# State space stage: half of the product with C taken by GpSimd in some of the states

## The chip, the cores and the metric

The kernel is one program on one core of one Trainium2 chip. The metric is the device time of one execution in microseconds, the median of the runs taken. One further execution was profiled; its span runs from the first to the last instruction, and its own device time is a little longer than the span.

## The reference, cut to what matters

The model is a decoder of four layers with twelve parts (attention, cross attention and feed forward in each). The part that the change touches is the attention of layer 2, a selective state space model on 64 sequences of 64 tokens, with 256 inner channels and N = 16 states per channel:

```
delta = softplus(dt @ w_dt)
deltaA = exp(delta[..., None] * A)
deltaBu = delta[..., None] * B[:, :, None, :] * u[..., None]
step(h, (a, bu)):  h = a * h + bu
y = einsum('bldn,bln->bld', hs, C) + u * D
out = (y * silu(res)) @ w_out
```

`y` is a sum over the 16 states of `hs * C`, where `C` is one row (a value per token and state) that is the same for all channels. The other eleven parts are not changed.

## The kernel before, in words

The twelve parts run one after the other as stages. The stage `state_space` (L2353 and on) has the channels on the 128 partitions, in two halves `c` = 0 and 1, and the tokens along the free dimension, in 8 groups `g` of GT = 512 tokens (NG = 8). Its main loop runs over M = 8 x 16 = 128 steps `m`, one for each group and state; `k = m % 16` is the state, and below "k = 4" means the step of that state in any group. All tiles are float32.

For each step and half the work is a chain over four engines:

- TensorE spreads the row of B over the partitions (`b_row`, into one PSUM bank) and the row of C (`c_row`, into two banks in turn), both at L2434.
- ScalarE copies the row of B into SBUF (`copy_b`, L2580, tile `bs`) and computes the decay exp(delta * A) of each half into a PSUM bank (`decay`, L2591).
- GpSimd multiplies `du` with the copied row of B (`inputs`, L2653, tile `bu`), once for each half.
- VectorE runs the recurrence (`scan`, L2716, tile `hs`) and multiplies its result with the row of C out of PSUM (`contribute`, L2724, tile `hc`), once for each half.
- TensorE adds `hc` over the 16 states in PSUM by multiplying with the identity (`accumulate`, L2456, two passes over float32).

GpSimd cannot be handed the row of C as it is, since that lies in PSUM; only `bs` is in SBUF. `bu`, `hs` and `hc` have two buffers each, by `m % 2`. So a scan of step m waits for the product of m - 2, a product waits for the sum of m - 2, and `c_row(m + 1)` waits until the products of step m - 1 have been taken. `decay(m + 1, c)` writes the bank that `scan(m, c)` reads and waits for it.

The order on each engine is written out by hand. In step m:

- TensorE: `accumulate(m-1, 0)`, `b_row(m+2)`, `c_row(m+1)`, `accumulate(m-1, 1)`, then work for other groups by k: at k = 0 to 3 the convolution of the next group (L2407, four matmuls in a step), at k = 4 the output projection of the group before (`output`, L163), at k = 5 and 6 two input projections (L2398), at k = 7 and 8 `projected` (L2417), at k = 9 and 10 `step_size` (L2425), at k = 13 a transposition, at k = 14 and 15 input projections.
- ScalarE: `decay(m+1, 0)`, `copy_b(m+2)`, `decay(m+1, 1)`, then by k: copies out of the shared bank, at k = 6 `silus` with a table load, at k = 9 to 11 the softplus with a table load, at k = 12 the scaling of a later group.
- GpSimd: `inputs(m+1)` for both halves, then at k = 2 `gated` (L2666), at k = 8 the norm of a later group (L661 to L673), at k = 9 `parts` (L2675 to L2680), at k = 12 `step_size` (L2658 and L2661, 1024 wide).
- VectorE: at k = 1 `skipped` of the group before (L2729), at k = 5 `residual` of the group before (L2734, waits for `output`), then `scan(m, 0)`, `contribute(m-1, 1)`, at k = 9 `below_high` (L2709), `scan(m, 1)`, `contribute(m, 0)`, at k = 7 statistics.

The work on later groups falls away in the last groups: group 6 has no norm, scaling, transposition or input projections of its own to prepare, and group 7 prepares nothing.

Of the kernel before, what the change touches and what calls it, by code (L numbers as in the profile page):

```python
# [18 lines left out]
ALU = mybir.AluOpType  # L19
# [7 lines left out]
GT = NT * P  # L27
# [2325 lines left out]
def state_space(nc, e, W):  # L2353

    N = 16
    M = NG * N
    use = ssm_order()  # L2360
    names = PN_SEMS + ("zeroed misc_mm misc_cp taps_done u_done res_done hi_done parts_own bc_parts relu_done sp_own sp_done "
                       "nb_raw nb_done dl_done du_done b_mm c_mm b_cp a_done bu_done hs_done hc_done acc_mm yo_done yr_done")
    with block_of(nc, "state_space", names) as (block, s):
        room = Room(e.arena)
        u_b, res_b, delta_b, du_b = (room.pair(2 * GT) for _ in range(4))
        u, res, delta, du = (lambda g, c, t=t: t(g)[:, c * GT:(c + 1) * GT] for t in (u_b, res_b, delta_b, du_b))
        bs = room.pair(GT)
        bu_t, hs_t, hc_t = (room.take(4 * GT) for _ in range(3))
        bu, hs, hc = (lambda m, c, t=t: t[:, (2 * (m % 2) + c) * GT:(2 * (m % 2) + c + 1) * GT] for t in (bu_t, hs_t, hc_t))
        xp_all, raw_u = room.take(2 * NB * (S + 3)), room.take(2 * GT)  # L2370
# [10 lines left out]
        @block.tensor  # L2381
        def _(pe):
            def take(step, g):
                if use[step, g] >= 1:
                    pe.wait_ge(s["misc_cp"], use[step, g])

            def turn(g):
                take("ln", g)
                for j in range(NT):
                    pe.wait_ge(s["ln_xn"], NT * g + j + 1)  # L2390
                    ins = pe.transpose(misc[:, j * P:(j + 1) * P], xn[:, j * D:(j + 1) * D], e.ident)
                ins.then_inc(s["misc_mm"], 1)

            def channels(step, g):
                m = int(step[1])
                take(step, g)
                pe.wait_ge(s["misc_cp"], use["ln", g] + 1)
                pe.matmul(misc, W("w_in")[:, m * P:(m + 1) * P], xnT, start=True, stop=True).then_inc(s["misc_mm"], 1)  # L2398

            def convolve(c, g, which):  # L2400
                if which[0] == 0:
                    take(("cv0", "cv1")[c], g)
                    pe.wait_ge(s["misc_cp"], use[("m0", "m1")[c], g] + 1)
                    if g == 0:
                        pe.wait_ge(s["taps_done"], 1)
                for i in which:
                    ins = pe.matmul(tiles(misc, NB), taps(c, i), xp(c)[:, :, i:i + S],  # L2407
                                    start=(i == 0), stop=(i == 3))
                if which[-1] == 3:
                    ins.then_inc(s["misc_mm"], 1)  # L2410

            def projected(step, g):
                k, lo, p0 = {"dt": (64, 0, 0), "bc": (32, 64, 64)}[step]
                take(step, g)
                pe.wait_ge(s["u_done"], 2 * (g + 1))
                for c in range(2):
                    ins = pe.matmul(misc[p0:p0 + k, :], W("w_x")[:, c * 96 + lo:c * 96 + lo + k], u(g, c),  # L2417
                                    start=(c == 0), stop=(c == 1))
                ins.then_inc(s["misc_mm"], 1)

            def step_size(step, g):
                c = int(step[1])
                take(step, g)
                pe.wait_ge(s["misc_cp"], use["dt", g] + 1)
                pe.matmul(misc, W("w_dt")[:, c * P:(c + 1) * P], dts, start=True, stop=True).then_inc(s["misc_mm"], 1)  # L2425

            def output(g):
                take("y", g)
                pe.wait_ge(s["yr_done"], 2 * (g + 1))
                project_out(pe, e, misc, [(u(g, c), W("w_out")[:, c * D:(c + 1) * D]) for c in range(2)],  # L2430
                            None).then_inc(s["misc_mm"], 1)

            def row_of(out, g, row):
                return pe.matmul(out, e.sel[:, row:row + 1].broadcast_to([96, P]), bcp(g), start=True, stop=True)  # L2434

            def b_row(m):
                if m < M:
                    pe.wait_ge(s["bc_parts"], m // N + 1)
                    if m >= 1:
                        pe.wait_ge(s["b_cp"], m)  # L2440
                    row_of(bbank, m // N, m % N).then_inc(s["b_mm"], 1)

            def c_row(m):
                if m < M:
                    pe.wait_ge(s["bc_parts"], m // N + 1)
                    if m >= 2:
                        pe.wait_ge(s["hc_done"], 2 * m - 2)
                    row_of(cbank(m), m // N, N + m % N).then_inc(s["c_mm"], 1)

            def accumulate(m, c):  # L2450
                if m >= 0:
                    g, k = m // N, m % N
                    if k == 0 and g >= 1:
                        pe.wait_ge(s["yo_done"], 2 * (g - 1) + c + 1)
                    pe.wait_ge(s["hc_done"], 2 * m + c + 1)
                    pe.matmul(acc(c), e.ident, hc(m, c), start=(k == 0), stop=(k == N - 1)).then_inc(s["acc_mm"], 1)  # L2456

            turn(0)
            channels("m0", 0)
            channels("m1", 0)  # L2460
            for c in range(2):
                convolve(c, 0, range(4))
            channels("m2", 0)
            channels("m3", 0)
            projected("dt", 0)
            projected("bc", 0)
            step_size("d0", 0)
            step_size("d1", 0)
            b_row(0)
            b_row(1)  # L2470
            c_row(0)
            turn(1)
            channels("m0", 1)
            channels("m1", 1)
            for m in range(M):
                g, k = m // N, m % N
                accumulate(m - 1, 0)
                b_row(m + 2)
                c_row(m + 1)
                accumulate(m - 1, 1)  # L2480
                if k == 4 and g >= 1:
                    output(g - 1)
                if g + 1 < NG:
                    if k < 4:
                        convolve(k // 2, g + 1, ((0, 1), (2, 3))[k % 2])
                    if k in (5, 6):
                        channels(("m2", "m3")[k - 5], g + 1)
                    if k in (7, 8):
                        projected(("dt", "bc")[k - 7], g + 1)
                    if k in (9, 10):  # L2490
                        step_size(("d0", "d1")[k - 9], g + 1)
                if g + 2 < NG:
                    if k == 13:
                        turn(g + 2)
                    if k in (14, 15):
                        channels(("m0", "m1")[k - 14], g + 2)
            accumulate(M - 1, 0)
            accumulate(M - 1, 1)
            output(NG - 1)

        @block.scalar
        def _(a):
# [72 lines left out]
            def copy_b(m):  # L2575
                if m < M:
# [2 lines left out]
                        a.wait_ge(s["bu_done"], 2 * (m - 1))  # L2579
                    a.activation(bs(m), bbank, ACT.Copy).then_inc(s["b_cp"], 1)  # L2580

            def decay(m, c):
                if m < M:
                    g, k = m // N, m % N
# [29 lines left out]
            for m in range(M):  # L2614
                g, k = m // N, m % N
                decay(m + 1, 0)
                copy_b(m + 2)
                decay(m + 1, 1)
                if g + 1 < NG:
                    if k in (1, 3):  # L2620
# [22 lines left out]
        def _(q):  # L2643
            def inputs(m):
                if m < M:
                    g, k = m // N, m % N
                    q.wait_ge(s["b_cp"], m + 1)
                    for c in range(2):
                        if k == 0:
                            q.wait_ge(s["du_done"], g + 1)  # L2650
                        if m >= 2:
                            q.wait_ge(s["hs_done"], 2 * (m - 2) + c + 1)
                        q.tensor_tensor(bu(m, c), du(g, c), bs(m), ALU.mult).then_inc(s["bu_done"], 1)  # L2653

            def step_size(g):
                q.wait_ge(s["relu_done"], 2 * (g + 1))
# [32 lines left out]
            for m in range(M):  # L2689
                g, k = m // N, m % N  # L2690
                inputs(m + 1)
                if k == 2 and g >= 1:
                    gated(g - 1)
                if k == 12 and g + 1 < NG:
# [9 lines left out]
        def _(v):  # L2704
# [6 lines left out]
            def scan(m, c):  # L2711
                v.wait_ge(s["a_done"], 2 * m + c + 1)
                v.wait_ge(s["bu_done"], 2 * m + c + 1)
                if m >= 2:
                    v.wait_ge(s["hc_done"], 2 * (m - 2) + c + 1)
                v.tensor_tensor_scan(hs(m, c), at(c), bu(m, c), 0.0, ALU.mult, ALU.add).then_inc(s["hs_done"], 1)  # L2716

            def contribute(m, c):
                if m >= 0:
                    v.wait_ge(s["hs_done"], 2 * m + c + 1)  # L2720
                    v.wait_ge(s["c_mm"], m + 1)
                    if m >= 2:
                        v.wait_ge(s["acc_mm"], 2 * (m - 2) + c + 1)
                    v.tensor_tensor(hc(m, c), hs(m, c), cbank(m), ALU.mult).then_inc(s["hc_done"], 1)  # L2724

            def skipped(g):
                for c in range(2):
                    v.wait_ge(s["acc_mm"], 2 * N * g + 2 * N - 1 + c)
                    v.scalar_tensor_tensor(out=u(g, c), in0=u(g, c), scalar=W("D")[:, c:c + 1], in1=acc(c),  # L2729
                                           op0=ALU.mult, op1=ALU.add).then_inc(s["yo_done"], 1)  # L2730

# [1117 lines left out]
```

## Time and profile before

| what | us |
|---|---|
| median of 3 runs | 3431.12 (3430.95 to 3440.71) |
| the profiled execution | 3430.59 |
| its span | 3428.8 |
| first and last scan of the stage | 1671.90 and 2201.0 |

The profile page gives the busy time of each engine over the whole span. The stage lies in the middle and takes about 530 us; its rows, by windows, groups and order of time, stand in the section below. In an order of time, a row has its start, its length, the instruction and, in brackets, the idle time of that engine before it with what ended it. Rows with x2 and more join neighbours of one kind.

### The profile page before, as it was taken

The numbers are of one execution on the slowest core, as the hardware profiler recorded it, in microseconds if no ns is written. First come the engines' busy times: TensorE is split into PE (matmuls) and PEld (weight loads), VectorE is DVE, ScalarE is ACT, GpSimd is POOL, SyncE is SP. The second block draws the span as 40 slices with busy tenths as digits, with TensorE's granted clock in tenths as the row PEclk, the third lists the DMA queues.
The fourth block names the chain that finished last, engine by engine and source line by source line (L and its number), as shares of the span: only waits on it lengthen the run. The fifth ranks groups of instructions, "written<-read, shape, count | busy, mean of one in ns | idle before, by whom it ended". The sixth has DMA issues, their size and how long they took to land. (4 is left out here: it accounts for less than half of the span.)

```text
span 3428.8 us, 72931 instructions
## 1 busy us (share of the span) xinstructions
PE 2747.4 (80%) x28239; PEld 1910.0 (56%) x28239; DVE 1912.3 (56%) x4174; ACT 1343.0 (39%) x2284; POOL 1431.3 (42%) x1553
## 2 busy tenths in 40 slices
PE   4987774998999979876788888694777999993394
PEld 2554443996777755655233333253446888872393
DVE  2554455114777756633388888745565665644123
ACT  3442231441111124312576677352233666651253
POOL 2545443223222145344387777633452111104555
PEclk8987786999999999798899999996788999995697
DMA  6000001660000010025000000000000000001375
GB/s 231 2 2 1 1 1 37 171 174 21 3 2 3 3 46 14 1 86 152 0 0 1 1 1 0 1 1 1 1 2 11 8 5 5 5 2 46 91 231 158
DMA packets 98054, 130.50 MB, mean 38 GB/s; under 512 B 31089, under 2 KB 76529, under 8 KB 97265
## 3 DMA queue, kind: packets, MB, share of 16 engines
q1 hardware_dynamic: 82768, 109.30, 10.7%
q0 software_dynamic: 7168, 14.78, 1.2%
q8 instruction: 227, 3.72, 0.5%
q10 hardware_dynamic: 7776, 1.77, 0.2%
q14 instruction: 115, 0.93, 0.1%
HBM read 103.64 MB, written 25.35 MB: 38 GB/s over the span
## 5 line engine op out<-in xcount | busy, mean ns | idle before, releaser
L661 POOL TENSOR_SCALAR arena<-arena 128x4 f32<-128x4 f32 x120 | 27.7, 231 | 1039.6 <-DVE arena L653 788.8
L2653 POOL TENSOR_TENSOR arena<-arena 128x512 f32<-128x512 f32 x256 | 318.6, 1273 | 121.2 <-ACT arena L2580 120.0
L2716 DVE TENSOR_TENSOR_SCAN arena<-ps,arena 128x512 f32<-128x512 f32 x256 | 310.9, 1215 | 58.4 <-ACT ps L2591 37.4
L2456 PE MATMUL ps<-arena,const_w 128*128 128x512 f32 x512 | 272.2, 614 | 13.5 <-DVE arena L2724 12.3
L163 PEld LDWEIGHTS ps<-L_attn_w,arena 128*128 128x128 f32 x1984 | 242.6, 194 | 53.2 <-issue 42.4
L163 PE MATMUL ps<-L_attn_w,arena 128*128 128x128 f32 x1984 | 258.7, 281 | 7.9 <-POOL arena L2666 3.4
L2591 ACT ACTIVATE ps<-arena,aneg 128x504 f32<-128x504 f32 x256 | 174.3, 681 | 103.7 <-DVE arena L2716 103.5
L429 ACT ACTIVATE arena<-ps 128x1024 f32<-128x1024 f32 x96 | 98.3, 1024 | 222.5 <-PE ps L331 222.5
L1782 PE MATMUL ps<-arena,L_attn_w 128*128 128x512 f32 x384 | 184.4, 617 | 0.9 <-ACT arena L742 0.9
L312 PE MATMUL ps<-arena 64*64 64x512 f32 x768 | 123.4, 718 | 63.4 <-POOL arena L485 63.4
L1850 ACT ACTIVATE arena<-ps,L_attn_w 128x512 f32<-128x512 f32 x64 | 44.0, 687 | 332.4 <-PE ps L1782 332.4
L2724 DVE TENSOR_TENSOR arena<-arena,ps 128x512 f32<-128x512 f32 x256 | 168.6, 659 | 0.0
L2434 PE MATMUL ps<-bcp,sel 96*128 96x512 bf16 x256 | 93.6, 387 | 71.6 <-DVE arena L2724 55.9
L2456 PEld LDWEIGHTS ps<-arena,const_w 128*128 128x128 f32 x512 | 91.7, 192 | 98.2 <-DVE arena L2724 60.3
L423 ACT ACTIVATE arena<-arena 128x1024 f32<-128x1024 f32 x96 | 101.3, 1055 | 97.4 <-DVE arena L551 97.3
L485 POOL TENSOR_TENSOR arena<-arena,const_w 128x1024 f32<-128x1024 f32 x64 | 120.7, 1897 | 35.4 <-PE ps L319 25.6
L345 PEld LDWEIGHTS ps<-arena 128*64 128x64 f32 x3072 | 107.4, 148 | 49.1 <-issue 27.1
L2246 DVE TENSOR_REDUCE arena<-arena 128x8 f32<-128x512 f32 x128 | 87.2, 681 | 83.9 <-ACT arena L2133 83.7
L163 PE MATMUL ps<-L_attn_w,ct_all 128*128 128x128 f32 x1024 | 131.0, 280 | 1.9 <-DVE arena L2262 1.9
L663 POOL TENSOR_TENSOR arena<-arena,mhalf 128x4 f32<-128x4 f32 x120 | 125.4, 1045 | 10.0
L687 POOL TENSOR_SCALAR arena<-x_all,arena 128x128 f32<-128x128 f32 x160 | 125.8, 799 | 7.3 <-POOL arena L663 6.2
L1093 DVE SCALAR_TENSOR_TENSOR arena<-ps,arena 128x64 f32 x108 | 30.7, 284 | 175.1 <-PE ps L912 166.6
(457 smaller groups left out, 6591.0 us busy)
## 6 DMA issues: line engine op xcount, KB each, us to landing
arena<-zone_w SPq DMA_DIRECT2D x54, 512.0 KB
arena<-pair_w SPq DMA_DIRECT2D x40, 578.0 KB
arena<-rt SPq DMA_DIRECT2D x24, 384.0 KB
pair_in<-pair_free SPq DMA_DIRECT2D x1, 5200.0 KB, 27.7
arena<-pair_in SPq DMA_DIRECT2D x40, 130.0 KB
arena<-ctx SPq DMA_DIRECT2D x16, 256.0 KB, 7.3
arena<-pair_out SPq DMA_DIRECT2D x16, 256.0 KB, 5.1
arena<-arena SPq DMA_DIRECT2D x108, 32.0 KB
```

What stands on the lines that cost most here:

```text
L163: ins = pe.matmul(out, src[:, j * P:(j + 1) * P], w, start=(i == 0), stop=(bias is None and i == len(chunks) - 1))
L312: ins = pe.matmul(tile(b2, h), q(g)[rows, t:t + S], kbd(i)[rows, :, b2 * S:(b2 + 1) * S], start=True, stop=rope)
L345: ins = pe.matmul(obank[b2 * S:(b2 + 1) * S, hp], pts(i)[:, hp * P + b2 * S:hp * P + (b2 + 1) * S], vbd(g)[:, 2 * j + b2, hp], start=True, ...
L485: p_.tensor_tensor(kbd(i), repeat(k(g)[:, j * P:(j + 1) * P], HH), spread(e.hmask8, P), ALU.mult).then_inc(s["kbd_done"], 1)
L663: q.tensor_tensor(rs[:, NT:2 * NT], rs[:, 0:NT], self.e.mhalf[:, 0:NT], ALU.pow).then_inc(self.rstd_s, 1)
L687: q.tensor_scalar(self.dst(g)[:, j * self.step:j * self.step + D], self.src(g)[:, j * D:(j + 1) * D], mv[:, 2 * j:2 * j + 1], rs[:, NT + j ...
L1782: pe.matmul(e.bank(i), W(w)[:, col], xnT(g), start=True, stop=True).then_inc(s["qkg_mm"], 1)
L2456: pe.matmul(acc(c), e.ident, hc(m, c), start=(k == 0), stop=(k == N - 1)).then_inc(s["acc_mm"], 1)
L2591: a.activation(tiles(at(c), NB)[:, :, 1:S], tiles(delta(g, c), NB)[:, :, 1:S], ACT.Exp, scale=e.aneg[:, c * N + k:c * N + k + 1]).then_inc ...
L2653: q.tensor_tensor(bu(m, c), du(g, c), bs(m), ALU.mult).then_inc(s["bu_done"], 1)
L2716: v.tensor_tensor_scan(hs(m, c), at(c), bu(m, c), 0.0, ALU.mult, ALU.add).then_inc(s["hs_done"], 1)
L2724: v.tensor_tensor(hc(m, c), hs(m, c), cbank(m), ALU.mult).then_inc(s["hc_done"], 1)
```

## The change

In the steps m > 0 whose state is in a list of five (0, 3, 5, 7, 14), the product of half 1 with C is taken by GpSimd and no longer by VectorE. Over 8 groups and without m = 0 these are 8 x 5 - 1 = 39 of the 256 products. For that ScalarE copies the row of C out of PSUM into a new pair of SBUF buffers `cs` (`copy_c`, between `copy_b` and the second `decay`). GpSimd takes the product of step m in its turn for step m + 1, after the two `inputs` of m + 2. TensorE adds such a product one step later than before, ahead of `accumulate(m-1, 0)`, and `c_row` then waits for the product of half 0 only. The number of sums is the same. VectorE's product of half 0 in such a step also waits for ScalarE's copy, which lets `c_row` rely on VectorE alone.

```diff
+    POOLED = (0, 3, 5, 7, 14)
+    by_pool = lambda m, c: c == 1 and m > 0 and m % N in POOLED
+    pooled = lambda m: sum(by_pool(i, 1) for i in range(m + 1))
+    products = lambda m: 2 * (m + 1) - pooled(m)
...
+        bs, cs_b = room.pair(GT), room.pair(GT)
+        cs = lambda m: cs_b(pooled(m))
...
             def c_row(m):
...
                     if m >= 2:
-                        pe.wait_ge(s["hc_done"], 2 * m - 2)
+                        pe.wait_ge(s["hc_done"], products(m - 2))
...
             for m in range(M):
                 g, k = m // N, m % N
+                if by_pool(m - 2, 1):
+                    accumulate(m - 2, 1)
                 accumulate(m - 1, 0)
                 b_row(m + 2)
                 c_row(m + 1)
-                accumulate(m - 1, 1)
+                if not by_pool(m - 1, 1):
+                    accumulate(m - 1, 1)
...
+            def copy_c(m):
+                if m < M and by_pool(m, 1):
+                    a.wait_ge(s["c_mm"], m + 1)
+                    if pooled(m) > 2:
+                        a.wait_ge(s["hp_done"], pooled(m) - 2)
+                    a.activation(cs(m), cbank(m), ACT.Copy).then_inc(s["cs_done"], 1)
...
                 copy_b(m + 2)
+                copy_c(m + 1)
                 decay(m + 1, 1)
...
+            def product(m):
+                if m >= 0 and by_pool(m, 1):
+                    q.wait_ge(s["hs_done"], 2 * m + 2)
+                    q.wait_ge(s["cs_done"], pooled(m))
+                    if m >= 2:
+                        q.wait_ge(s["acc_mm"], summed[m - 2, 1])
+                    q.tensor_tensor(hc(m, 1), hs(m, 1), cs(m), ALU.mult).then_inc(s["hp_done"], 1)
...
                 inputs(m + 1)
+                product(m - 1)
...
             def contribute(m, c):
-                if m >= 0:
+                if m >= 0 and not by_pool(m, c):
                     v.wait_ge(s["hs_done"], 2 * m + c + 1)
                     v.wait_ge(s["c_mm"], m + 1)
+                    if by_pool(m, 1):
+                        v.wait_ge(s["cs_done"], pooled(m))
```

## Rows read from the trace of the kernel before

**Rows 1.** Windows: k = 1 to 4 of group 3; group 3 whole; group 7.
```profile
core 0: us, PE busy (x) PEld busy (x) DVE busy (x) ACT busy (x) POOL busy (x), PEclk, DMA share, GB/s
1877.50:1896.87 19.37, 18.66 (x60) 9.24 (x61) 16.58 (x20) 9.64 (x16) 14.33 (x11) 1.00 0.00 1
1875.56:1942.78 67.22, 57.96 (x153) 22.68 (x152) 59.08 (x77) 47.28 (x74) 51.44 (x44) 0.97 0.00 1
2144.45:2205.00 60.55, 44.24 (x113) 15.11 (x113) 58.32 (x71) 27.97 (x45) 38.83 (x31) 1.00 0.00 1
```
**Rows 2.** Groups of instructions of the stage (1675 to 2200 us).
```profile
L2653 POOL TENSOR_TENSOR arena<-arena 128x512 f32<-128x512 f32 x253 | 314.9, 1273 | 121.0 <-ACT arena L2580 120.0
L2724 DVE TENSOR_TENSOR arena<-arena,ps 128x512 f32<-128x512 f32 x252 | 166.0, 659 | 0.0
L2580 ACT ACTIVATE arena<-ps 128x512 f32<-128x512 f32 x126 | 73.5, 583 | 11.1 <-PE ps L2434 10.3
```
**Rows 3.** VectorE in order of time, start and length first, k = 1 of group 3.
```profile
1881.43 0.66 DVE L2724 TENSOR_TENSOR arena<-arena,ps 128x512 f32<-128x512 f32 x1
1882.01 1.21 DVE L2716 TENSOR_TENSOR_SCAN arena<-ps,arena 128x512 f32<-128x512 f32 x1
```
**Rows 4.** TensorE in order of time, k = 1 and k = 4 of group 3.
```profile
1881.15 0.38 PE L2434 MATMUL ps<-bcp,sel 96*128 96x512 bf16 x1
1882.24 0.38 PE L2434 MATMUL ps<-bcp,sel 96*128 96x512 bf16 x1 [0.71 <-DVE arena L2724]
1882.45 1.02 PE L2456 MATMUL ps<-arena,const_w 128*128 128x512 f32 x2
...
1894.06 1.02 PE L2456 MATMUL ps<-arena,const_w 128*128 128x512 f32 x2
1894.92 1.95 PE L163 MATMUL ps<-L_attn_w,arena 128*128 128x128 f32 x16
```
**Rows 5.** VectorE at k = 5 of the same group, before the residual.
```profile
1896.90 0.69 DVE L2734 TENSOR_TENSOR x_all<-ps,x_all 128x512 f32<-128x512 f32 x1 [2.83 <-PE ps L163]
```
**Rows 6.** ScalarE from k = 6 to 8, and at k = 11.
```profile
1902.81 0.58 ACT L2580 ACTIVATE arena<-ps 128x512 f32<-128x512 f32 x1
1903.89 0.69 ACT L2591 ACTIVATE ps<-arena,aneg 128x504 f32<-128x504 f32 x1 [0.51 <-DVE arena L2716]
1905.01 0.69 ACT L2538 ACTIVATE arena<-ps,L_attn_w 128x512 f32<-128x512 f32 x1 [0.42 <-PE ps L2398]
...
1926.63 0.67 ACT L2591 ACTIVATE ps<-arena,aneg 128x504 f32<-128x504 f32 x1
```
**Rows 7.** GpSimd from k = 8 of group 3 to k = 1 of group 4.
```profile
1911.64 2.50 POOL L2653 TENSOR_TENSOR arena<-arena 128x512 f32<-128x512 f32 x2 [5.67 <-ACT arena L2580]
...
1916.27 2.49 POOL L2653 TENSOR_TENSOR arena<-arena 128x512 f32<-128x512 f32 x2
...
1922.09 7.42 POOL L2653 TENSOR_TENSOR arena<-arena 128x512 f32<-128x512 f32 x6
1929.81 2.36 POOL L2658 TENSOR_TENSOR arena<-arena 128x1024 f32<-128x1024 f32 x1 [0.31 <-ACT arena L2573]
...
1934.56 9.95 POOL L2653 TENSOR_TENSOR arena<-arena 128x512 f32<-128x512 f32 x8
```
**Rows 8.** VectorE before the scans of k = 11 and k = 14.
```profile
1923.44 1.22 DVE L2716 TENSOR_TENSOR_SCAN arena<-ps,arena 128x512 f32<-128x512 f32 x1 [0.74 <-ACT ps L2591]
...
1935.93 1.22 DVE L2716 TENSOR_TENSOR_SCAN arena<-ps,arena 128x512 f32<-128x512 f32 x1 [0.71 <-issue]
```
**Rows 9.** TensorE at k = 0 of the next group, group 4.
```profile
1943.23 1.02 PE L2456 MATMUL ps<-arena,const_w 128*128 128x512 f32 x2
...
1945.80 0.59 PE L2407 MATMUL ps<-arena,pq 128*128 128x512 f32 x1
```
**Rows 10.** TensorE before the last output within the loop, group 7, k = 4.
```profile
2160.56 0.38 PE L2434 MATMUL ps<-bcp,sel 96*128 96x512 bf16 x1
...
2162.48 1.95 PE L163 MATMUL ps<-L_attn_w,arena 128*128 128x128 f32 x16
```

## What the change was predicted to do

> **What bounds the kernel now.** I read the busy time by windows first. In one group of 67.22 us VectorE is busy 59.08, TensorE 57.96, GpSimd 51.44 and ScalarE 47.28 [rows 1]. So VectorE is the busiest, but it idles some 8 us in each group, and TensorE is only 1.1 us behind it. What matters is which engine holds the work at each k. The order of time shows four places:
>
> - k = 0 to 4: TensorE. It has 18.66 us of matmuls in 19.37 us [rows 1]; the rest is one wait of 0.71 us in front of the row of C [rows 4]. At the end VectorE has stood idle for 2.83 us before `residual`, which needs TensorE's `output` [rows 5].
> - k = 5 to 8: ScalarE, through the second `decay` of k = 7, the copy L2538, the two Silu with their table loads and the next `decay` (from 1903.89 on [rows 6]).
> - k = 8 to 11: GpSimd. From 1911.64 to 1929.5 it works without a pause [rows 7]. Its product `bu` of k = 11 is the first of the six from 1922.09 and ends near 1923.35; the scan that needs it starts at 1923.44 after an idle of 0.74 [rows 8]. The view names ScalarE as releaser, but the product ends 0.09 us before the scan, so I put it down to GpSimd.
> - k = 12 to 14: ScalarE and GpSimd together. GpSimd waits 0.31 us for the softplus [rows 7], and the scan of k = 14 starts at 1935.93, 0.71 late [rows 8], when the first product from 1934.56 has ended (near 1935.83).
>
> Everywhere else, and in group 7, VectorE is the bound.
>
> **What is taken from VectorE.** A product is 0.66 us long, but the next scan starts 0.58 after it (1881.43 to 1882.01 [rows 3]). 39 products times 0.58 are 22.6 us. That is the most that VectorE can give; it counts only where VectorE is the bound or where its end starts one of the chains above.
>
> **What is put on the others.** A GpSimd product of this size, both inputs in SBUF, is the form of L2653: 1.27 us long [rows 2], one every 1.24 (eight in 9.95 [rows 7]). The copy of C has the form of L2580, 0.58 long [rows 2]; the following instruction starts 0.50 after it, which I take as its price. TensorE gets no more matmuls. The trace has no GpSimd product beside the new waits; its bounds are 1.24 (alone) and 1.27 plus 0.15 for the handover that a row of C shows after a product of VectorE (its end 1882.09, start 1882.24 [rows 3, 4]). I take 1.24, and 0.15 once where TensorE waits for it.
>
> **k = 0 to 4, on TensorE.** In step k = 1 `c_row(2)` waits for the product of k = 0, half 1. That is now GpSimd's, and `c_row` asks for half 0 alone, ready long before. The row can start 0.21 after that of B (the distance of the next matmul behind such a row, 1882.24 to 1882.45) instead of 1.09 after it: 0.87 gained [rows 4]. In step k = 4 the sum of k = 3, half 1 (1894.06 to 1894.92 [rows 4]) goes behind `output` into step 5: 0.86 gained. Together 1.73 in each of groups 1 to 6, since the 2.83 us of idle [rows 5] show that VectorE is not in the way. For the same reason the 0.58 of k = 0 and of k = 3 on VectorE bring nothing here. The sum of k = 0 only moves behind the convolution and ahead of the same projection.
>
> **k = 5 to 8, on ScalarE.** The product of k = 5 no longer stands ahead of the second scan of k = 6, which ends 0.58 sooner. The copy of C for k = 7 falls in this gap: `copy_b` starts at 1902.81, the copy at 1903.31, `decay` at 1903.81 instead of 1903.89 [rows 6]. So only 0.08 is won there. But L2538 behind it waited 0.42 for TensorE [rows 6], where the sum of k = 5 stood ahead of its matmuls and now does not; it follows 0.60 after `decay`, at 1904.41 instead of 1905.01. Gain 0.60 in groups 0 to 6.
>
> **k = 8 to 14, on GpSimd.** The product of k = 7 is issued behind `inputs` of k = 9 and ahead of the norm, `inputs` of k = 10, `parts` and `inputs` of k = 11. GpSimd has no pause in this stretch [rows 7], so all of it is late by 1.24, and with it the scan of k = 11. That of k = 7 on VectorE (0.58) is lost in the wait. Up to the softplus 0.22 comes back: the second `decay` at 1926.63 [rows 6] starts 0.22 after the scan that it could follow, and the 0.31 us of GpSimd's wait [rows 7] absorb the same. Loss 1.02 in groups 0 to 5. In group 6 there is no norm (some 2.1 us between 1914.14 and 1916.27 [rows 7]) and the product is covered.
>
> **k = 14 to the next k = 0, from GpSimd to TensorE.** Leaving aside the shift of GpSimd itself, six `bu` start at 1934.56 and on [rows 7], then the product of k = 14: it ends at 1934.56 + 6 x 1.24 + 1.27 = 1943.27. Then 0.15 of handover, the moved sum of k = 14 (0.86), the first sum of k = 15 (0.86), the two rows (0.43), the second sum (0.86): the convolution starts at 1946.43, against 1945.80 now [rows 9]. Loss 0.63 in groups 0 to 5. VectorE's own 0.58 of k = 14 would have been 1.2 us ahead of that and is lost. The handovers of k = 0, 3 and 5 come while GpSimd is ahead and cost nothing; without that lead (some 3 us at k = 2 and more at 5) each would cost TensorE up to 1.24.
>
> **Groups 6 and 7.** In group 6 the stretch from k = 8 to the next k = 1 is bound by VectorE and ScalarE: with the product covered I take a gain of 1.0 from k = 5 on: ScalarE's 0.60, and an estimated 0.4 of the two times 0.58 that VectorE is spared at k = 7 and 14. In group 7 TensorE has pauses. `output` follows the rows of B and C directly: the row of B moves up 0.58 with the product of k = 0, to 2159.98, `output` to 2160.41 instead of 2162.48 [rows 10]: 2.07 sooner. VectorE, spared 0.58 twice on its way and idle before `residual` in this group too, can follow. Then 0.58 for each of k = 5, 7 and 14: 1.74. Together 3.8.
>
> **The sum.** Groups 1 to 6 gain 6 x 1.73 = 10.4 on TensorE. Groups 0 to 5 lose from k = 5 on 1.02 + 0.63 - 0.60 = 1.05 each, 6.3. Group 6 gains 1.0 there and group 7 gains 3.8. In all 10.4 - 6.3 + 1.0 + 3.8 = 8.9 us gained. The profiled execution's 3430.6 becomes 3421.7 (its span of 3428.8 becomes 3419.9), and since the median of the runs is 0.5 above the profiled time the forecast is **3422** us, 0.26% less.
>
> **A rule of the skill.** The Trainium skill (Perfetto Trace Analysis, section Optimizing Scalar/DVE Operations) warns that GpSimd and VectorE share an SBUF read port, so moving work between these two may not help. By this trace VectorE's products take 0.659 on average and GpSimd's 1.273 while both run side by side through the whole stage [rows 2], so no hold-up shows; each of VectorE's large operations has one input in PSUM. The rule stands among the rivals.
>
> **The rivals.**
>
> - VectorE is the bound after all, as the window's busy times suggest [rows 1]. Then nearly all 39 x 0.58 us count, with TensorE's gain beside them: 15 to 22 us, to 3409 to 3416. For it: the highest busy time. Against it: the idle before `residual` and k = 11, where GpSimd has no room [rows 5, 7]. The same skill page (section Identifying the Most-Contended Engine) says to go by occupancy and would side with this rival.
> - GpSimd covers nothing and TensorE gives less. If the 1.73 of k = 0 to 4 is given back because the sums moved behind the convolution are late, groups 0 to 5 pay their 1.05 and only groups 6 and 7 gain: 6.3 - 4.8 = 1.5 slower, near 3432.6, and from 0 to 5 us faster with a part of the 1.73. It decides where TensorE's gain in a group falls under 0.25 us ((6.3 - 4.8) / 6).
> - Slower: GpSimd's products hold VectorE up. If a product on GpSimd that reads `hs` and `cs` stops VectorE for its length, 39 x 1.27 = 49.5 are added, and with the 8.9 gained the time is near 3472. It decides where a product holds VectorE up by more than 0.23 us (8.9 / 39). Against it: [rows 2, 3]. The skill's port rule would give this time.
> - The change does less than it says. If the waits keep `c_row` behind half 1, TensorE's 0.87 is missing and the time is 5 us higher, near 3427; it shares the chance of small gains below.
>
> **How the numbers follow.** Forecast (5 to 14 us faster) 0.50; VectorE the bound 0.19; less of TensorE's gain, 0 to 5 us faster 0.19; no gain to 8 us slower 0.08; port 0.04. A gain under 0.3%, 10.3 us, cannot be told from none here. Of the forecast's 0.50 some 0.22 lies above 10.3, with the 0.19 that makes faster 0.41; slower 0.05 (the port and the far end of the case before it); the same 0.54. The range goes from 3410 to 3431: all of the forecast, most of VectorE as bound, and the small gains.
>
> **What will show it.** Right: the idle before `residual` still near 3 us while it comes earlier; no pause of 0.71 at k = 1 on TensorE; the scan of k = 11 waiting longer than 0.74; a pause on TensorE at k = 0 before the sum of k = 14; a group of some 66.5 us, and group 7 some 4 us shorter. Wrong: VectorE's scan or product longer than 1.22 or 0.66; a group of 65 us or less; or TensorE waiting for GpSimd at k = 2, 5 or 9.

## The result and the profile after

The changed kernel takes 3421.41 us in the median (3413.88 to 3430.42, 17 runs) against 3431.12 (3421.92 to 3442.14, 17 runs); the ratio is 0.9971, 95% interval 0.9961 to 0.9981. The profiled span is 3419.5 us (3428.8 before). The stage, from the first to the last start of a scan, went from 529.1 to 520.1 us: 9.0 of the 9.3 us in the span. The scans' own row in the trace of the changed kernel (durations in ns, then first and last start):

```profile
L2753 DVE TENSOR_TENSOR_SCAN arena<-ps,arena x256: 1195/1217/1225, 1669.5 to 2189.6; 128x512 f32<-128x512 f32 x128
```

By windows, the same two stretches as in [rows 1], group 3 whole and group 7 (columns as there):

```profile
1871.76:1938.19 66.43, 57.36 (x152) 22.76 (x152) 56.40 (x73) 49.20 (x80) 57.47 (x49) 0.97 0.00 1
2136.18:2193.00 56.82, 44.27 (x115) 16.87 (x115) 55.06 (x65) 29.93 (x50) 46.64 (x37) 0.97 0.00 0
```

A group fell from 67.22 to 66.43 us. VectorE lost 2.7 us of work (59.08 to 56.40) and GpSimd gained 6.0 (51.44 to 57.47), so GpSimd is now the busiest. By groups of instructions, the lines that answer to [rows 2], with the two new ones (L2687 the product on GpSimd, L2605 the copy of C):

```profile
L2679 POOL TENSOR_TENSOR arena<-arena 128x512 f32<-128x512 f32 x253 | 315.0, 1272 | 69.0 <-ACT arena L2598 66.5 <-DVE arena L2753 0.5
L2763 DVE TENSOR_TENSOR arena<-arena,ps 128x512 f32<-128x512 f32 x215 | 142.2, 662 | 0.0
L2687 POOL TENSOR_TENSOR arena<-arena 128x512 f32<-128x512 f32 x39 | 49.6, 1271 | 1.4 <-DVE arena L2753 1.4
L2605 ACT ACTIVATE arena<-ps 128x512 f32<-128x512 f32 x39 | 23.0, 589 | 0.1
```

The new operations have the prices of their nearest forms, and VectorE's product is 662 ns long against 659. The 178 products of VectorE that lie by nine tenths or more beside a GpSimd instruction take 662 ns in the mean, and the 14 that lie by less than a tenth beside one take 663. So GpSimd does not hold them up.

TensorE at k = 1, k = 4, k = 9 and at the next k = 0, the answer to [rows 4, 9]:

```profile
1878.53 0.60 PE L2445 MATMUL ps<-bcp,sel 96*128 96x512 bf16 x2
...
1890.14 0.60 PE L2445 MATMUL ps<-bcp,sel 96*128 96x512 bf16 x2
1890.58 1.95 PE L163 MATMUL ps<-L_attn_w,arena 128*128 128x128 f32 x16
...
1910.42 1.98 PE L2470 MATMUL ps<-arena,const_w 128*128 128x512 f32 x4 [0.81 <-POOL arena L2687]
...
1939.27 1.98 PE L2470 MATMUL ps<-arena,const_w 128*128 128x512 f32 x4 [1.15 <-POOL arena L2687]
```

The rows of B and C follow each other without the 0.71 us pause, the projection follows the rows with no sum between, and at k = 0 TensorE waits 1.15 us for GpSimd's product of k = 14. At k = 9 it waits 0.81 us for that of k = 7. VectorE still idles before `residual` [rows 5]:

```profile
1892.56 0.69 DVE L2773 TENSOR_TENSOR x_all<-ps,x_all 128x512 f32<-128x512 f32 x1 [2.86 <-PE ps L163]
```

ScalarE from k = 6 to 8 [rows 6], now without a gap from the copy of C (L2605) on:

```profile
1898.46 0.58 ACT L2598 ACTIVATE arena<-ps 128x512 f32<-128x512 f32 x1
1898.94 0.59 ACT L2605 ACTIVATE arena<-ps 128x512 f32<-128x512 f32 x1
1899.42 0.68 ACT L2616 ACTIVATE ps<-arena,aneg 128x504 f32<-128x504 f32 x1
1900.02 0.68 ACT L2556 ACTIVATE arena<-ps,L_attn_w 128x512 f32<-128x512 f32 x1
```

GpSimd from k = 8 [rows 7], with the product of k = 7 at 1909.11 and that of k = 14 at 1937.92:

```profile
1906.66 2.49 POOL L2679 TENSOR_TENSOR arena<-arena 128x512 f32<-128x512 f32 x2 [4.77 <-ACT arena L2598]
1909.11 1.26 POOL L2687 TENSOR_TENSOR arena<-arena 128x512 f32<-128x512 f32 x1
...
1918.29 7.40 POOL L2679 TENSOR_TENSOR arena<-arena 128x512 f32<-128x512 f32 x6
1925.81 2.36 POOL L2692 TENSOR_TENSOR arena<-arena 128x1024 f32<-128x1024 f32 x1
...
1937.92 1.30 POOL L2687 TENSOR_TENSOR arena<-arena 128x512 f32<-128x512 f32 x1
```

The scan of k = 11 on VectorE [rows 8] now waits three times as long, and its wait ends as GpSimd's first `bu` from 1918.29 does:

```profile
1919.65 1.22 DVE L2753 TENSOR_TENSOR_SCAN arena<-ps,arena 128x512 f32<-128x512 f32 x1 [2.28 <-issue]
```

### The profile page after: what moved, and what is told of

Its sections match the earlier page's. It is cut to its first block and busy times, and to the rows that moved or that the text cites. A ratio compares the mean times of both kernels' runs of the same rounds, so it can differ in the third digit from the quotient of the medians.

```text
span 3419.5 us, 73046 instructions
## 1 busy us (share of the span) xinstructions
PE 2742.3 (80%) x28239; PEld 1912.6 (56%) x28239; DVE 1892.5 (55%) x4135; ACT 1357.4 (40%) x2323; POOL 1475.3 (43%) x1592
## 5 line engine op out<-in xcount | busy, mean ns | idle before, releaser
L2763 DVE TENSOR_TENSOR arena<-arena,ps 128x512 f32<-128x512 f32 x217 | 143.5, 662 | 0.0
L163 PEld LDWEIGHTS ps<-L_attn_w,ct_all 128*128 128x128 f32 x1024 | 123.0, 194 | 9.3 <-DVE arena L2262 4.3
```

Source lines behind the costliest of these rows:

```text
L163: ins = pe.matmul(out, src[:, j * P:(j + 1) * P], w, start=(i == 0), stop=(bias is None and i == len(chunks) - 1))
```

## The experiments

Two measures are used: the stage, from the first to the last start of a scan, and a whole group (from the first scan of group 3 to that of group 4). Both repeat far better than the time of the whole kernel does. Kernels without a ratio in the table were run once, for their profile.

```
                          stage    group 3   ratio to the kernel before, 95% interval
before                    529.1    67.22
changed                   520.1    66.43     0.9971 (0.9961 to 0.9981)
changed, again            519.5    66.47     0.9972 (0.9962 to 0.9981)
only 7                    534.7    68.20     1.0024 (1.0013 to 1.0034)
only 0, 3                 516.4    65.49
one sum moved             522.7    66.35
changed, 7 twice          532.7    67.63
changed, 3 twice          522.7    66.44
0, 3, 5, 14               512.1    64.99     0.9942 (0.9925 to 0.9958)
0, 3, 5                   508.6    64.40     0.9945 (0.9927 to 0.9963)
0, 3, 4, 5                505.2    63.80     0.9924 (0.9908 to 0.9941)
0, 3, 4, 5, output first  518.3    66.00
0, 2, 3, 4, 5, same       533.7    68.91
and 7, 10, 13 in group 7  533.6    68.90     1.0004 (0.9993 to 1.0015)
```

**TensorE's part, without GpSimd.** The kernel before, with one line moved:

```diff
-                accumulate(m - 1, 1)
                 if k == 4 and g >= 1:
                     output(g - 1)
+                accumulate(m - 1, 1)
```

> The kernel before, with nothing given to GpSimd; only TensorE's sum of k = 3, half 1, is issued behind the output projection instead of ahead of it. Theory of chains: 0.86 less in each group with an output at k = 4: a group 66.4, the stage 523.1. Rival (VectorE is the bound): no change, 529.1.

A group took 66.35: 0.87 less, though no engine does less work. VectorE's idle before `residual` went from 2.83 [rows 5] to 1.97 in this kernel:

```profile
1881.04 0.69 DVE L2734 TENSOR_TENSOR x_all<-ps,x_all 128x512 f32<-128x512 f32 x1 [1.97 <-PE ps L163]
```

So TensorE is the bound from k = 0 to 4. Moving the place of one sum brings a steady group more than the whole change does (0.87 against 0.79), and makes the stage 6.4 us shorter, of the change's 9.0. Of these, 6.1 lie in groups 1 to 7; the rest is in group 0, which the moved line does not touch.

**Only k = 0 and 3.**

```diff
-    POOLED = (0, 3, 5, 7, 14)
+    POOLED = (0, 3)
```

> Only the products of k = 0 and 3 go to GpSimd (15 of 256). Theory of chains: TensorE's two gains of 0.87 and 0.86 and nothing else: a group 65.5 us, the stage 529.1 - 6 x 1.73 - 2.1 in group 7 = 516.7, shorter than with all five states (520.1). Rival (VectorE is the bound): 15 x 0.58 = 8.7 shorter, 520.4, a group 66.1, longer than with five states.

65.49 measured, 65.5 expected, and a stage of 516.4 against 516.7: TensorE's two gains are 1.73 us. The kernel with 15 products moved has a shorter stage than the one with 39.

**Only k = 7.** The list is `(7,)`.

> Only the product of k = 7, half 1, goes to GpSimd (8 of 256). Measure: the stage from its first to its last scan, 529.1 us before, and a whole group, 67.22 before. Theory of chains: nothing is gained up to k = 8, GpSimd is late by 1.24 in its full stretch, 0.22 comes back at the softplus: a group is 1.02 longer (68.2), the stage 5 us longer (534), the kernel slower although VectorE has less to do. Rival (VectorE is the bound): 8 x 0.58 = 4.6 us shorter, 524.5. Port rival (a GpSimd product holds VectorE up for 1.27): 8 x 1.27 less 4.6, 5.6 longer, but with scans or products of VectorE that are longer in the rows.

A group is 0.98 longer, the stage 5.6, and the kernel 0.24% slower, although VectorE does less. Its products and scans kept their lengths (659 ns, and 1214 against 1215), so it is no hold-up at a port. GpSimd's first `bu` of k = 11 starts 11.65 us behind the pair of k = 9, where it was 10.45 [rows 7]. GpSimd in this kernel, with the product (L2688) behind the first pair and `inputs` of k = 11 at 1924.62, and VectorE's scan that waits for it:

```profile
1912.97 2.50 POOL L2680 TENSOR_TENSOR arena<-arena 128x512 f32<-128x512 f32 x2 [5.67 <-ACT arena L2599]
1915.43 1.26 POOL L2688 TENSOR_TENSOR arena<-arena 128x512 f32<-128x512 f32 x1
...
1924.62 7.40 POOL L2680 TENSOR_TENSOR arena<-arena 128x512 f32<-128x512 f32 x6
```
```profile
1925.97 1.22 DVE L2754 TENSOR_TENSOR_SCAN arena<-ps,arena 128x512 f32<-128x512 f32 x1 [2.29 <-issue]
```

**A product twice, at k = 7 and at k = 3.** In the changed kernel, into a tile that nobody reads (the other kernel has `== 3` in place of `== 7`):

```diff
+                    if m % N == 7:
+                        q.tensor_tensor(again(m), hs(m, 1), cs(m), ALU.mult)
```

> The changed kernel, but in k = 7 GpSimd takes its product twice, once more into a tile that nobody reads. Theory of chains: GpSimd is full from k = 8 on, so 1.24 more in each of groups 0 to 5 and up to 1 in group 6: a group 67.7 instead of 66.4, the stage 520.1 + 7.4 to 8.4 = 528. Rival (GpSimd has room, 51 of 67 us busy): no change, 520.1. Port rival: 8 x 1.27 = 10.2 more, 530, also with the second product at another k.

> The changed kernel, but in k = 3 GpSimd takes its product twice, once more into a tile that nobody reads. Theory of chains: at k = 3 to 5 GpSimd is ahead by 2 to 5 us, so nothing changes: a group 66.4, the stage 520.1. Port rival (a GpSimd product holds VectorE up for 1.27): 8 x 1.27 = 10.2 more, 530, less what the idle before the residual takes in.

At k = 7 the second product costs 1.20 in group 3, its full price. The whole cost was 12.6 us, not 8. In groups 0, 1 and 5 the step k = 12 is 0.42 longer on top of the 1.20, and in groups 6 and 7 the step k = 10 is 1.66 and 1.64 longer: 4.6 us in all. TensorE waits for GpSimd's product of k = 7 in every group, 2.03 or 2.04 us in groups 0 to 6. But only in those five groups did the granted clock fall to 0.50, the 1.2 GHz level, in the sums behind that wait; in groups 2 to 4 it stayed at 1.00. Groups 2 and 5 of this kernel:

```profile
1840.71 1.98 PE L2472 MATMUL ps<-arena,const_w 128*128 128x512 f32 x4 [2.03 <-POOL arena L2691]
...
2043.63 3.68 PE L2472 MATMUL ps<-arena,const_w 128*128 128x512 f32 x4 [2.04 <-POOL arena L2691]
```

At k = 3 groups 1 to 6 did not move (66.42 to 66.45): GpSimd's time is free there. On the port this kernel says little, since the second product (1893.76 to 1895.03 in group 3) falls into VectorE's idle time before `residual`. The lengths of VectorE's instructions beside GpSimd's decide that question.

The 2.6 us that the stage still lost lie in groups 0 and 7. In group 0 TensorE waits 1.63 us for the product of k = 3 instead of 0.41. In group 7 nearly all of it is one step, k = 8, which took 4.90 instead of 2.83. TensorE waited for a GpSimd product, as it does again at 2175.09 without loss. But behind the first wait the granted clock was 0.51, four sums took 3.68 instead of 1.99, and the row of B came late by that (TensorE of the kernel with k = 3 twice):

```profile
2164.00 0.60 PE L2447 MATMUL ps<-bcp,sel 96*128 96x512 bf16 x2
2166.71 3.68 PE L2472 MATMUL ps<-arena,const_w 128*128 128x512 f32 x4 [2.11 <-POOL arena L2691]
...
2175.09 1.99 PE L2472 MATMUL ps<-arena,const_w 128*128 128x512 f32 x4 [2.12 <-POOL arena L2691]
```

**Without k = 7; only 0, 3 and 5; and 0, 3, 4 and 5.**

> The changed kernel without k = 7 in the list (0, 3, 5, 14: four states, 31 products). Theory of chains: GpSimd's 1.24 at k = 8 goes, and ScalarE has no copy of C ahead of the second decay of k = 7, so that 0.60 becomes 1.10: a group 67.2 - 1.73 - 1.10 + 0.63 = 65.0, the stage near 511. Rival (VectorE is the bound): 8 products of 0.58 come back to it, the stage 524.7.

> Only k = 0, 3 and 5 (23 products). Theory of chains: TensorE's 1.73 and ScalarE's 1.10 and neither loss: a group 64.4, the stage 508.2. Rival (VectorE is the bound): 23 x 0.58 = 13.3 shorter than before, 515.8, and less than with k = 14 as well.

> k = 0, 3, 4 and 5 (31 products). Theory of chains: the product of k = 4 is taken off VectorE right after the residual, at the head of the chain over ScalarE to k = 8, and GpSimd has room there: 0.58 more in each group than with 0, 3 and 5, a group 63.8, the stage 503.6. Rival: if TensorE's projection of k = 6 is what ScalarE waits for, nothing more than with 0, 3 and 5: 508.2.

Groups of 64.99, 64.40 and 63.80 against 65.0, 64.4 and 63.8 expected. The stages were 512.1, 508.6 and 505.2 against 511, 508.2 and 503.6. The last miss lies in group 0, which with k = 4 in the list took 69.16 instead of 68.26; why was not looked into. The differences give each term by itself: k = 14 costs 0.59 in a group (64.99 - 64.40), k = 5 gives 1.09 where no copy of C stands in the way (65.49 - 64.40), k = 4 gives 0.60. ScalarE of the kernel with 0, 3 and 5 shows why k = 5 is worth 1.09 there: L2557 follows the second `decay` at once.

```profile
1893.47 0.58 ACT L2599 ACTIVATE arena<-ps 128x512 f32<-128x512 f32 x1
1893.96 0.69 ACT L2617 ACTIVATE ps<-arena,aneg 128x504 f32<-128x504 f32 x1
1894.58 0.67 ACT L2557 ACTIVATE arena<-ps,L_attn_w 128x512 f32<-128x512 f32 x1
```

With 0, 3, 4 and 5 the kernel takes 3406.09 us against 3434.14 for the one before on the same chip, by the table's ratio 0.76% less: the best that was found, with a stage 15 us shorter than the changed kernel's.

**The projection ahead of everything in k = 4.** On top of 0, 3, 4 and 5:

```diff
+                if k == 4 and g >= 1:
+                    output(g - 1)
                 if by_pool(m - 2, 1):
                     accumulate(m - 2, 1)
```

> k = 0, 3, 4 and 5 on GpSimd, and TensorE issues the output projection at the head of step k = 4, ahead of the sums and rows of that step. Theory of chains: the projection needs the shared bank free, which ScalarE's copy of the last convolution gives some 0.36 before its place now, so only 0.36 of the 1.29 us in front of it is gained: a group 63.4, the stage 505.2 - 7 x 0.36 = 502.7. Rival (TensorE alone holds it): 1.29 in each of 7 groups, the stage 496.

Both were wrong: 66.00 and a stage of 518.3, or 2.2 us more in a group. `residual` did come earlier, by 0.25 (a step k = 4 of 5.56 instead of 5.81). But the rows of B and C now stood behind the projection, and ScalarE's copies of both wait for them ahead of its second `decay`. ScalarE and VectorE of this kernel:

```profile
1892.98 0.60 ACT L2599 ACTIVATE arena<-ps 128x512 f32<-128x512 f32 x1 [2.64 <-PE ps L2445]
1893.47 0.59 ACT L2606 ACTIVATE arena<-ps 128x512 f32<-128x512 f32 x1
1893.95 1.29 ACT L2617 ACTIVATE ps<-arena,aneg 128x504 f32<-128x504 f32 x2
```
```profile
1894.67 1.22 DVE L2754 TENSOR_TENSOR_SCAN arena<-ps,arena 128x512 f32<-128x512 f32 x1 [0.95 <-ACT ps L2617]
```

That makes the step k = 5 longer by 1.06. The other 1.39 come at k = 7, after GpSimd's product of k = 4 was late too and held up TensorE:

```profile
1897.44 1.98 PE L2470 MATMUL ps<-arena,const_w 128*128 128x512 f32 x4 [1.27 <-POOL arena L2688]
```

My expectation had followed the projection and not what it was moved past.

**k = 2 as well, and more in group 7.** The list becomes `(0, 2, 3, 4, 5)`, and for group 7 `(0, 2, 3, 4, 5, 7, 10, 13)`.

> As the one with the output projection at the head of k = 4, with k = 2 given to GpSimd too (0, 2, 3, 4, 5). Theory of chains: the sum of k = 2, half 1, falls behind the projection and the last convolution comes 0.86 sooner: a group 62.6, the stage near 497. Rival: GpSimd is full from k = 1 to 5 (19.7 of some 20 us) and becomes the bound there: a group of 63.4 or more.

> As the one with 0, 2, 3, 4 and 5, and in the last group also k = 7, 10 and 13. Theory of chains: in the last group VectorE is the bound and GpSimd has room, so 3 x 0.59 = 1.8 less: the stage near 495, 34 us less than before, the kernel near 0.990 of the one before. Rival: TensorE waits for each of GpSimd's products in that group and nothing is gained: 497.

The group is far longer than either said, 68.9, and not by GpSimd's total, as the rival had it. Three copies of C in a row need two `cs` buffers, GpSimd was late with the product that frees one, and ScalarE stood for it with everything behind: its copy L2606, then the convolution's copy L2557, on which TensorE's projection waits. ScalarE and then TensorE of the kernel without the extra states:

```profile
1891.74 0.60 ACT L2606 ACTIVATE arena<-ps 128x512 f32<-128x512 f32 x1 [1.52 <-POOL arena L2688]
1892.24 0.68 ACT L2617 ACTIVATE ps<-arena,aneg 128x504 f32<-128x504 f32 x1
1892.84 0.68 ACT L2557 ACTIVATE arena<-ps,L_attn_w 128x512 f32<-128x512 f32 x1
```
```profile
1893.58 3.68 PE L163 MATMUL ps<-L_attn_w,arena 128*128 128x128 f32 x16 [2.04 <-ACT arena L2557]
```

The waits by themselves account for 1.3 us over the 66.00 without k = 2: groups 4 and 6, where TensorE kept its full clock, took 67.29 and 67.28. The other 1.6 us are the clock's, told in the last section. The three more states in group 7 gave nothing (533.6 against 533.7), as that run's rival had it: TensorE waited 2.12, 1.80 and 2.02 us for the products of k = 7, 10 and 13.

**The changed kernel again.**

> The changed kernel once more, beside the others of this call. The stage 520.1 and a group 66.4 again, within 0.1; the whole time may differ by several us, as far as the parts ahead of the stage do.

66.47 and 519.5: the stage is 0.6 shorter, more than the 0.1 that I had allowed. In the step k = 3 of group 7 the first profile has 3.83 and this one 3.43. TensorE waits for GpSimd's product of k = 0 equally long in both, but in the first the granted clock in the four sums behind was 0.50 (first the changed kernel, then the repeat):

```profile
2144.02 3.62 PE L2470 MATMUL ps<-arena,const_w 128*128 128x512 f32 x4 [2.06 <-POOL arena L2687]
```
```profile
2139.68 1.96 PE L2470 MATMUL ps<-arena,const_w 128*128 128x512 f32 x4 [2.07 <-POOL arena L2687]
```

## Why the prediction was right

The time was forecast as 3422 and is 3421.4; the stage was to lose 8.9 us and lost 9.0. That the whole time came within 1 us is luck, since the runs of the changed kernel lie 16 us apart; the stage and its parts are the test. By its own steps, in a steady group:

- k = 0 to 4 on TensorE, 1.73 gained: right. The two parts together were 1.73 in the kernel with only 0 and 3, and the moved sum alone was 0.87.
- k = 5 to 8 on ScalarE, 0.60 gained: 0.63 (13.56 to 12.93 from scan to scan). In group 0 only 0.21 came.
- k = 8 to 14 on GpSimd, 1.02 lost: 0.99 (24.84 to 25.83), and 0.98 with k = 7 alone.
- k = 14 to the next k = 0, 0.63 lost: 0.59. With k = 0 to 4 it makes 28.80 to 27.67 from the scan of k = 14 to that of the next k = 5, 1.13 gained against 1.10.
- The handovers at k = 0, 3 and 5 were to cost nothing. In groups 1 to 6 that held. In group 7 TensorE waits there for up to 2.06 us; by itself that cost nothing either, and with the lower clock behind it 0.40 reached VectorE.
- TensorE waiting for GpSimd at k = 9 was named as a sign of being wrong, and it does wait, 0.81 us in groups 0 to 6. It cost nothing that shows, as the stretch lost 0.99 and not more than 1.02.
- Groups 6 and 7. From k = 5 of group 6 to its end and the next k = 0 the gain was 1.2 instead of 1.0. From there on it was 3.45 instead of 3.8 in the first profile and 3.86 in the repeat: the missing 0.4 is TensorE's clock, for which the prediction has no term.

The errors are small and partly cancel: a steady group gained 0.79, where my terms made 0.68, and group 7 gave less than its term. The rivals fell: VectorE as the bound by k = 7 alone, where less work on it made the kernel slower, and by the moved sum, which took nothing from it; a smaller gain on TensorE by the 1.73; the port by the unchanged lengths. That last is shown only for VectorE's scan and product, each with one input in PSUM; one with both inputs in SBUF was not tried.

The busy times of the windows pointed the wrong way. VectorE was the busiest engine before, yet 39 products of 0.58 us, 22.6 in all, brought 9.0, while the order on TensorE alone brought 6.1. So going by occupancy (the Trainium skill, Perfetto Trace Analysis, section Identifying the Most-Contended Engine) gives the wrong engine from k = 0 to 4 and from k = 8 to 14. What the same page of the Trainium skill says in its section Optimization Strategy, that the most-contended engine can change over time, is what this trace bears out.

## What to carry to other kernels

When several engines share a repeated step, cut the period at the points where the busiest one idles and ask which engine holds the work in each stretch; then price a move by the stretch in which it lands, not by the engine's total. Work taken off an engine ahead of someone else's wait is worth nothing, and work put on an engine in its full stretch costs its whole length (1.20 of 1.24 us here at k = 11, of which 0.2 came back later) even where that engine has 16 us of idle time in the period. An instruction moved in an in-order queue has to be judged by what it is moved past.

## What was not expected

TensorE's clock. With k = 2 in the list as well TensorE stood idle for 2.04 us in front of the projection in group 3, which then took 3.68 us instead of 1.95. By windows of that kernel (columns as in [rows 1]), the stretch before, the projection and what follows:

```profile
1882.00:1891.53 9.53, 9.53 (x25) 3.88 (x23) 8.92 (x10) 6.33 (x11) 8.52 (x7) 1.00 0.01 3
1893.58:1897.07 3.49, 3.49 (x16) 3.49 (x17) 1.17 (x2) 0.52 (x1) 1.75 (x2) 0.51 0.01 2
1897.07:1900.00 2.93, 2.93 (x9) 1.36 (x9) 1.82 (x2) 0.77 (x2) 0.10 (x1) 1.00 0.00 0
```

The granted clock is 0.51, the 1.2 GHz level, through the projection and 1.00 on both sides. A pause made by a wait elsewhere can thus cost more behind it, here 1.6 us of the group (68.9 against 67.29). But it does not always. In groups 4 and 6 of the same kernel the same pause left the clock at 1.00:

```profile
1962.48 2.05 PE L163 MATMUL ps<-L_attn_w,arena 128*128 128x128 f32 x16 [2.05 <-ACT arena L2557]
```

With k = 7 or k = 3 twice, and in the changed kernel against its repeat, pauses of 2.03 to 2.12 us went both ways too. With a pause of 0.78 in front of the projection (the projection ahead, without k = 2) the granted clock was 1.00 in all six groups. What decides between the two for equal pauses, these runs do not show.

The clock also moves the start of the stage. TensorE enters it at the lower level. Where the level rose 9.5 us after the first scan (the changed kernel again) the step k = 2 of group 0 took 4.06 us, at 10.3 us (the kernel before) 4.45, and at 11.1 us (0, 3, 5, 14) 4.82. So stages of different runs compare to some 0.8 us and no better, and the steady groups are the finer measure.

And where the scatter of the kernel's time lies: the work ahead of the stage is the same in all kernels here, yet in the profiled runs the first scan started anywhere from 1659.0 us (one sum moved) to 1678.4 us (0, 3, 5, 14), while the steady groups (1 to 5) of a kernel agree within 0.03 us. Those with k = 7 twice or k = 2 are aside, and so is group 1 with only k = 7 (68.37 against 68.21). A change of a few microseconds is seen in its own stage long before it is seen in the total. What scatters ahead of the stage was not looked into.
